# Causal and narrow attention on halves of the array's rows, with per-head waits and moved products

## What is computed

```
x = x + _L0_attn_ref(_layernorm(x), ...)    # causal, 16 heads of 8
...
x = x + _L1_attn_ref(_layernorm(x), ...)    # causal, keys and values from 32 latents
...
x = x + _L2_xattn_ref(_layernorm(x), ctx, ...)   # 512 queries on 77 keys, scores clipped
...
x = x + _L3_xattn_ref(_layernorm(x), ctx, ...)   # 512 queries on 77 keys
...
# the core of each
scores = jnp.einsum('bqhd,bkhd->bhqk', q * scale, k) + bias   # bias: later keys masked, causal ones only
attn_weights = jax.nn.softmax(scores, axis=-1)
attn_output = jnp.einsum('bhqk,bkhd->bqhd', attn_weights, v)
```

## Time and profile before

| | |
|---|---|
| median of 3 runs | 1516.36 us (1514.69 to 1518.23) |
| the profiled execution | 1514.06 us, its span 1512.2 us |
| PE busy | 1418.1 us, 94% of the span |
| DVE / ACT / POOL busy | 955.7 / 674.3 / 346.3 us |
| mean granted clock | 0.979 |

### The profile page before, as it was taken

One profiled execution on the slowest core, in us unless ns is written; L12 is line 12 of the kernel. 1 busy time (PEld: TensorE's weight loads), 2 busy tenths in 40 slices (PEclk: granted clock), 3 DMA queues, 4 the chain that ended last, 5 costly groups with the idle time before them and its releaser, 6 DMA issues. The chain is left out here.

```text
span 1512.2 us, 27644 instructions
## 1 busy us (share of the span) xinstructions
PE 1418.1 (94%) x10790; PEld 890.2 (59%) x10790; DVE 955.7 (63%) x1911; ACT 674.3 (45%) x1651; POOL 346.3 (23%) x372
## 2 busy tenths in 40 slices
PE   8999999999999998998998988989998999999996
PEld 6665574644666656566786857674444555664434
DVE  6676372644366655645668337668888887677755
ACT  4776244324267654524420324533556777750002
POOL 4000031100101010010421202027777665600001
PEclk9999899999899999999999999999999999999998
DMA  3000000421000000000011302010110101399980
GB/s 126 2 2 2 3 2 0 154 72 42 15 2 2 2 2 17 1 20 4 2 60 78 126 11 83 2 43 15 42 42 28 30 15 26 64 223 254 253 213 15
DMA packets 24062, 79.13 MB, mean 52 GB/s; under 512 B 4808, under 2 KB 6646, under 8 KB 23552
## 3 DMA queue, kind: packets, MB, share of 16 engines
q1 hardware_dynamic: 23072, 74.26, 18.0%
q10 hardware_dynamic: 864, 3.15, 0.8%
HBM read 72.11 MB, written 1.08 MB: 48 GB/s over the span
## 5 line engine op out<-in xcount | busy, mean ns | idle before, releaser
L193 PE MATMUL psum<-ident 128*128 128x128 f32 x1392 | 175.7, 284 | 13.0 <-DVE var L143 5.6
L193 PEld LDWEIGHTS psum<-ident 128*128 128x128 f32 x1392 | 167.4, 198 | 20.9 <-DVE var L143 6.6
L475 ACT ACTIVATE pt<-psum,quad_max 128x128 f32<-128x128 f32 (+3 forms) x256 | 133.6, 525 | 68.4 <-DVE quad_max L513 64.4
L184 POOL TENSOR_TENSOR rstd<-var,minus_half 128x4 f32<-128x4 f32 x30 | 30.7, 1023 | 574.5 <-DVE var L143 539.4
L513 DVE TENSOR_REDUCE quad_max<-psum 128x1 f32<-128x128 f32 (+3 forms) x256 | 113.5, 485 | 67.7 <-PE psum L404 67.4
L2733 PE MATMUL psum<-pt,slots 128*128 128x512 f32 x256 | 115.0, 604 | 3.5 <-DVE pt L2886 2.9
L2712 PE MATMUL psum<-slots,xn_t 128*128 128x512 f32 x256 | 113.9, 605 | 3.1 <-DVEq L2857 3.1
L2471 ACT ACTIVATE p<-psum,duo_max 128x512 f32<-128x512 f32 x128 | 86.9, 683 | 43.2 <-DVE duo_max L2506 43.1
L2801 ACT ACTIVATE pt<-psum,p 128x64 f32<-128x64 f32 x256 | 58.0, 393 | 72.5 <-POOL wide L2943 43.7
L2733 PEld LDWEIGHTS psum<-pt,slots 128*128 128x128 f32 x256 | 48.0, 192 | 69.6 <-issue 50.8
L2506 DVE TENSOR_REDUCE duo_max<-psum 128x1 f32<-128x512 f32 x128 | 82.3, 684 | 10.0 <-PE psum L2382 7.8
(11 more groups left out here) (505 smaller groups left out, 2794.1 us busy)
## 6 DMA issues: line engine op xcount, KB each, us to landing
pt<-scratch_out_gates SPq DMA_DIRECT2D x32, 256.0 KB, 12.2
heads<-scratch_out_gates SPq DMA_DIRECT2D x24, 256.0 KB, 14.5
slots<-in_s_l0f SPq DMA_DIRECT2D x8, 514.0 KB, 3.3
wide<-scratch_gates SPq DMA_DIRECT2D x8, 512.0 KB, 7.5
slots<-in_s_l3v SPq DMA_DIRECT2D x8, 512.0 KB, 3.3
context_v<-scratch_out_gates SPq DMA_DIRECT2D x16, 256.0 KB, 18.3
slots<-in_s_l3o ACTq DMA_DIRECT2D x6, 512.0 KB, 10.2
weights<-in_w_l1a SPq DMA_DIRECT2D x1, 2624.0 KB, 9.4
```

The lines of the kernel that those rows point to most:

```text
L193: nc.tensor.matmul(m.ps[bank][:, 0:P], m.ident[:, :], m.ident[:, :], start=True, stop=True, skip_group_check=True)
L475: nc.scalar.activation(m.quad_p[:, i % 2, g, 0:keys], m.ps[g][:, 0:keys], ACT.Exp, bias=m.quad_max[:, i % 2, g:g + 1], accum_out=sum_colum ...
```

## The change

- Two heads of a pair are now each on 64 of the 128 rows (half_rows): head g of the loop lies at rows 64 * (g % 2), with keys copied twice (head_keys, latent_t), once with the odd 32-row quarters zeroed by ScalarE and once with the even ones by VectorE. HEAD_OF maps the loop's order to the heads' places in the output.
- The mask comes as four bf16 products on 64 rows and 64 columns a pair instead of two on all rows and 128 columns.
- Transposes are made of 64 rows each, the two halves into two banks; a step turns two key blocks of four heads (16 instructions) or one (8). VectorE copies out the lower half, ScalarE the upper. The second pair of key blocks is turned after the scores of heads 0 and 1 of the next set.
- Each head's scores wait for that head's exponential alone.
- The spreading product (share) and the projection (ahead) move from behind the values to between the scores of a pair's first and second head: share between heads 2 and 3 of set i when i-3 ended a group, the projection between heads 0 and 1 of set i+1. ScalarE's copy of the projection moves from after head 1's exponential to the end of its step.
- Narrow stages: score tiles of 64 rows, with keys of eight heads in keys_own, and 16 transposes of 64 rows instead of 8 full ones.
- Three constants more are loaded (later, parity, rows8), and one more is cast by ScalarE.

```diff
@@ -392,38 +406,71 @@
     return m.ps[T_BANKS[bank]]
-def quad_scores(nc, pe, m, a, n, heads, q, k, q_ready):
+def quad_scores(nc, pe, m, a, n, heads, q, k, q_ready, between=None):
     b, j, qt = quad_set(n)
     q_ready(pe, b, j, qt)
-    wait(pe, m.quad_exp, GROUP * (a.sets0 + n) - (GROUP - 1 - heads[1] if n else 0))
     keys = (qt + 1) * P
     for g in heads:
+        wait(pe, m.quad_exp, GROUP * (a.sets0 + n) - (GROUP - 1 - g if n else 0))
         nc.tensor.matmul(m.ps[g][:, 0:keys], q(g, b, j, qt), k(g, b, keys), start=True, stop=False)
-    for g in heads:
-        nc.tensor.matmul(m.ps[g][:, keys - P:keys], m.ident_bf[:, :], m.future_bf[:, :], start=False,
-                         stop=True).then_inc(m.quad_scores, 1)
+        if between and g == heads[0]:
+            between()
+    for part in range(2):
+        for g in heads:
+            own, at = half_rows(g % 2), keys - P + 64 * part
+            last = nc.tensor.matmul(m.ps[g][:, at:at + 64], m.later_bf[own, part, :], m.ident_bf[own, own], start=False,
+                                    stop=part == 1)
+            if part == 1:
+                last.then_inc(m.quad_scores, 1)
+def quad_turn(nc, pe, m, a, n, pair):
+    banks = [turn_bank(pe, m, a.turn[n, 2 * pair + half]) for half in range(2)]
+    blocks = pair_keys(n, pair)
+    for kt in blocks:
+        for g in range(GROUP):
+            for half in range(2):
+                own, at = half_rows(half), (kt % 2 * GROUP + g) * 64
+                last = nc.tensor.transpose(banks[half][:, at:at + 64], m.quad_p[own, n % 2, g, kt * P:(kt + 1) * P],
+                                           m.ident[own, own])
+                if kt == blocks[-1] and g == GROUP - 1:
+                    last.then_inc(m.quad_turned, 1)
 def quad_tensor(nc, pe, m, a, q, k, values, q_ready, v_ready, project, ramp):
+    def share(group):
+        pe.wait_ge(m.quad_spread, m.inverted0[a.name] + group + 1)
+        bank = turn_bank(pe, m, a.share[group])
+        for t in range(NQ):
+            last = nc.tensor.matmul(bank[:, t * P:(t + 1) * P], m.quad_wide[:, group % 2, t, :], m.ident[:, :],
+                                    start=True, stop=True)
+        last.then_inc(m.quad_turned, 1)
+    def ahead(group):
+        project(turn_bank(pe, m, a.ahead[group]), group).then_inc(m.quad_turned, 1)
     quad_scores(nc, pe, m, a, 0, (0, 1), q, k, q_ready)
-    for i in range(SETS + 2):
+    for i in range(SETS + 3):
+        shared = (lambda: share((i - 3) // a.group_sets)) if a.ends_group(i - 3) else None
         if i < SETS:
-            quad_scores(nc, pe, m, a, i, (2, 3), q, k, q_ready)
+            quad_scores(nc, pe, m, a, i, (2, 3), q, k, q_ready, shared)
+        elif shared:
+            shared()
         if i < len(RAMP):
             ramp(i)
         n = i - 1
         if 0 <= n < SETS:
-            for kt in range(n % NQ + 1):
-                bank = turn_bank(pe, m, a.turn[n, kt])
-                for g in range(GROUP):
-                    if kt == 0:
-                        pe.wait_ge(m.quad_exp, GROUP * (a.sets0 + n) + g + 1)
-                    last = nc.tensor.transpose(bank[:, g * P:(g + 1) * P], m.quad_p[:, n % 2, g, kt * P:(kt + 1) * P],
-                                               m.ident[:, :])
-                last.then_inc(m.quad_turned, 1)
+            pe.wait_ge(m.quad_exp, GROUP * (a.sets0 + n) + GROUP)
+            quad_turn(nc, pe, m, a, n, 0)
         if i + 1 < SETS:
-            quad_scores(nc, pe, m, a, i + 1, (0, 1), q, k, q_ready)
+            quad_scores(nc, pe, m, a, i + 1, (0, 1), q, k, q_ready,
+                        (lambda: ahead((i + 2) // NQ)) if a.projects(i - 1) else None)
+        if 0 <= n < SETS and key_pairs(n) > 1:
+            quad_turn(nc, pe, m, a, n, 1)
         n = i - 2
         if 0 <= n < SETS:
...
             last.then_inc(m.quad_values, 1)
             if a.ends_group(n):
                 nc.tensor.matmul(m.ps[O_BANK][:, 0:P], m.zeros[:, :], m.ident[:, :], start=False, stop=True,
                                  skip_group_check=True).then_inc(filled(m, f"{a.name}o{group}"), 1)
-                pe.wait_ge(m.quad_spread, m.inverted0[a.name] + group + 1)
-                bank = turn_bank(pe, m, a.share[group])
-                for t in range(NQ):
-                    last = nc.tensor.matmul(bank[:, t * P:(t + 1) * P], m.quad_wide[:, group % 2, t, :], m.ident[:, :],
-                                            start=True, stop=True)
-                last.then_inc(m.quad_turned, 1)
-        if a.projects(i):
-            group = (i + 3) // NQ
-            project(turn_bank(pe, m, a.ahead[group]), group).then_inc(m.quad_turned, 1)
-def quad_take(copy, eng, m, a, n, kt):
+def quad_take(copy, eng, m, a, n, u):
+    pair, half = divmod(u, 2)
+    blocks = pair_keys(n, pair)
     wait(eng, m.quad_values, a.sets0 + n - 1)
-    bank = turn_filled(eng, m, a.turn[n, kt])
-    copy(m.quad_pt[:, n % 2, kt, :], bank).then_inc(m.quad_taken[a.turn[n, kt][0]], 1)
+    bank = turn_filled(eng, m, a.turn[n, u])
+    copy(m.quad_pt[:, n % 2, blocks[0]:blocks[-1] + 1, :].rearrange("p k (g a q) -> p (k g) a q", a=2, q=64)[:, :, half, :],
+         bank[:, 0:len(blocks) * S // 2].rearrange("p (k q) -> p k q", q=64)).then_inc(m.quad_taken[a.turn[n, u][0]], 1)
...
@@ -464,27 +506,27 @@
     for i in range(SETS + 3):
         n = i - 1
-        taken = [kt for kt in range(n % NQ + 1) if kt % 2 == 1] if 0 <= n < SETS else []
+        taken = [2 * pair + 1 for pair in range(key_pairs(n))] if 0 <= n < SETS else []
         if i < SETS:
             b, j, qt = quad_set(i)
             keys = (qt + 1) * P
             if i >= 2:
-                act.wait_ge(m.quad_turned, a.turn[i - 2, (i - 2) % NQ][2] + 1)
+                act.wait_ge(m.quad_turned, a.turn[i - 2, 2 * key_pairs(i - 2) - 1][2] + 1)
             for g in range(GROUP):
                 act.wait_ge(m.quad_negmax, GROUP * (a.sets0 + i) + g + 1)
                 nc.scalar.activation(m.quad_p[:, i % 2, g, 0:keys], m.ps[g][:, 0:keys], ACT.Exp,
                                      bias=m.quad_max[:, i % 2, g:g + 1],
-                                     accum_out=sum_column(g, b, j, qt)).then_inc(m.quad_exp, 1)
+                                     accum_out=sum_column(HEAD_OF[g], b, j, qt)).then_inc(m.quad_exp, 1)
                 if g == 1 and a.ends_group(i - 3):
                     take_output((i - 3) // a.group_sets)
-                if g == 1 and a.projects(i - 1):
-                    take_ahead((i + 2) // NQ)
                 if g >= 2 and taken:
                     quad_take(copy, act, m, a, n, taken.pop(0))
         elif a.ends_group(i - 3):
             take_output((i - 3) // a.group_sets)
-        for kt in taken:
-            quad_take(copy, act, m, a, n, kt)
+        for u in taken:
+            quad_take(copy, act, m, a, n, u)
+        if i < SETS and a.projects(i - 1):
+            take_ahead((i + 2) // NQ)
...
@@ -529,10 +571,11 @@
             dve.wait_ge(m.quad_exp, GROUP * (a.sets0 + n) + GROUP)
             invert(n // a.group_sets).then_inc(m.quad_inverted, 1)
         if 0 <= n < SETS:
-            for kt in range(0, n % NQ + 1, 2):
-                quad_take(nc.vector.tensor_copy, dve, m, a, n, kt)
+            quad_take(nc.vector.tensor_copy, dve, m, a, n, 0)
         if i + 1 < SETS:
             maxima(i + 1, (0, 1))
+        if 0 <= n < SETS and key_pairs(n) > 1:
+            quad_take(nc.vector.tensor_copy, dve, m, a, n, 2)
...
-            nc.scalar.activation(dst[:, j * S:(j + 1) * S], bank[:, :], ACT.Identity,
-                                 bias=bias).then_inc(emptied(m, f"{name}{j}"), 1)
+    for j in range(2):
+        bank = read(m, act, f"l0q{j}")
+        nc.scalar.activation(m.q_t[:, j * S:(j + 1) * S], bank[:, :], ACT.Identity,
+                             bias=w["bq"]).then_inc(emptied(m, f"l0q{j}"), 1)
+    for j in range(2):
+        bank = read(m, act, f"l0k{j}", 1)
+        nc.scalar.activation(m.head_keys[0][:, j * S:(j + 1) * S], bank[:, :], ACT.Identity, bias=w["bk_even"],
+                             scale=m.parity[:, 0:1]).then_inc(emptied(m, f"l0k{j}"), 1)
     def take_output(b):
...
     head_queries(0)
+    for j in range(2):
+        copied(m, dve, f"l0k{j}")
+        bank = read(m, dve, f"l0k{j}", 1)
+        nc.vector.tensor_scalar(m.head_keys[1][:, j * S:(j + 1) * S], bank[:, :], m.parity[:, 1:2], w["bk_odd"], ALU.mult,
+                                ALU.add).then_inc(emptied(m, f"l0k{j}"), 1)
     for j in range(2):
         bank = read(m, dve, f"l0v{j}")
...
@@ -1697,9 +1762,9 @@
                 else:
                     wait(pe, m.negmax_ready, a.s0 + k - 1)
                 for x in range(2):
-                    rows = own(2 * half + x)
+                    rows = slice(64 * x, 64 * x + 64)
                     last = nc.tensor.matmul(m.ps[2 * (k % 2) + x][:, 0:GROUP * SC], m.q_t[rows, b * S + qt * P:b * S + (qt + 1) * P],
```

(14 more changed lines are left out.)

117 lines of the change are left out of this document (78 added, 39 removed).

## The result

The changed kernel takes **1508.30 us** (median of 4 runs, 1506.73 to 1509.97) against 1516.59 before (4 runs): ratio 0.9946, 95% interval [0.9929, 0.9963]. It is faster, but by 8 us, not by the forecast 34, and the time lies above the range (1467 to 1499). A second set gave 1510.77 (12 runs) and 0.9969 [0.9947, 0.9990]. The profiled execution took 1508.48, span 1506.7, mean granted clock 0.972 (0.979 before).

A forecast was written before the change was run, and what follows sets the result against it. TensorE's sequence was taken to bound the causal stages until other engines and the score-bank chain do. First causal stage -17.6, second -7.8, narrow -6.6 and -2.4, together -34.4, gave 1482 us; forecast 1474 to 1490, range 1467 to 1499.

The forecast's parts named there:

- TensorE's own work: First causal stage, TensorE's round: transposes 2.75, scores 4.8, mask 1.0, value products 3.2, together 11.8 us.
- What is late next: First causal stage: VectorE 10.7, ScalarE 11.6, one-bank chain 11.0; longest by set 12.6, so a round of 12.7 us.
- rival B: Causal stages: the chain and the queues bind, rounds of 13.9 and 17.0 us, time 1498; chance 0.18.
- Spreading and projection between the heads: Second causal stage: heads can't run side by side, +0.65 and +0.87; round 15.6 us on TensorE, 16.4 forecast.
- Rival C: Causal stages: pairs come apart, each costing its streams twice, +4.36 and +2.8 us a round, time 1524; chance 0.04.
- Starts: Start of both causal stages: next projection also waits for VectorE's copy of the keys, some 0.8 us at each.
- Head by head: Causal stages: waiting for each head's exponential separately costs TensorE nothing alone, since the mask needs both heads' exponentials anyway.
- Narrow stages: Half transposes shorten the later stage's round from 5.90 to 4.95 us, -6.6 in all; the earlier stage -2.4.
- The clock: Sign of being wrong: granted clock, 1.00 in both stretches of the table, falls with TensorE's new waits; no size given.

The follow-up runs named there:

- cuts on different engines: Kernel with both scores of a pair before spreading and projection; maxima, value products, ScalarE's copies cut to 128 keys: 1482.68, 1492.04, 1502.78 us alone, 1468.66 together.
- moving VectorE's copy: Kernel with both scores of a pair before spreading and projection, plus VectorE's first-turn copy between the maxima of heads 2 and 3: 1495.88 us, ratio 0.9878.
- three moves made for this loop: Both scores before spreading and projection, plus VectorE's copy between maxima; value products behind scores of heads 2 and 3; or both: 1495.88, 1498.24, 1525.03 us.
- both scores ahead: Changed kernel with spreading and projection issued behind both scores of their pair instead of between the heads: 1499.56 us, ratio 0.9906; again 1502.05, 0.9909.

## Why the prediction was wrong, point by point

**TensorE's own work: right.** 16 half transposes take 0.53 (109.91 to 110.44, the next group's start), forecast 0.55. The round without its waits, 13.86 - 1.58 - 0.6, is 11.7; forecast 11.8. The rule of the Trainium skill (TensorE: Matmul & The Clock Gate, LDWEIGHTS) that was set aside, by which alone 16 loads would take an estimated 1.7 us, does not give the price of these loads on alternating halves.

**What is late next: the step that failed.** TensorE's work was right and its waits were not: forecast 12.7 - 11.8 = 0.9 a round, measured 2.2. The prediction read the chain at one bank, scores, maximum, exponential, summed it to 11.0, took 12.6 as the sum of the longest by set, and went for 12.7 with a ceiling of 13.9 "a quarter of the idle share more". But the loop that exists doesn't stay in one bank: it takes value products and turns out of TensorE's queue, copies out of VectorE's and ScalarE's, 8.0 us on TensorE's side, 4.1 on VectorE's and 1.8 or so on ScalarE's, and comes to 13.85. TensorE waits for it: 1.19 and 0.39 for VectorE's copies, 0.6 for ScalarE's exponential. It can probably be written down from the code's four queues and the durations of the earlier trace rows; that was not tried. Eight rounds 1.16 too long are 9.3 us. It is **rival B** in this stage, to its number of 13.9; in the second stage its 17.0 was passed (17.57), and its total of 1498 would still have been missed.

**Spreading and projection between the heads: price right, place wrong.** I costed the split at 1.52 and counted it on TensorE, with 0.8 for waits on top (16.4). Measured it is 1.52 too, but on top of a round that was 16.05 and not 14.9: 8 x 1.17 = 9.4 us missed. That the two figures agree is partly luck. The forecast is TensorE's lost overlap alone; the measured one is a whole round's, in which VectorE and ScalarE stand idle for up to 2.78. Rival C's mechanism, a pair that comes apart because its second head waits, shows in one pair of eight in the first stage (118.58 to 120.15) and costs nothing there: with one wait for the pair it stays together behind a wait of 0.54, and the round is 13.89.

**Starts: right.** +1.1 in the first stage in this profile, some +0.8 on average, and +0.9 in the second; forecast +0.8 each. **Head by head: right** (0.03 a round).

**Narrow stages: right at full clock.** 2.5 gained (forecast 2.4) and 5.7 (forecast 6.6; the round is 5.11, forecast 4.95). **The clock: named as a sign of being wrong, and not priced.** In the profiled run it kept 6.2 us of the narrow gain (0.8 more is the forecast's own excess). In the first causal stage it cost an estimated 1.9, against the same kernel's second profile, which has falls of its own: 0.85 in one round (14.88 against 14.03) and 1.05 from the last round's first exponential to the next normalization (28.52 against 27.47). In the untouched stage behind it cost 1.4.

The sum by spans: forecast -34.4, measured -5.5, so 28.9 are missing. The first causal stage has 12.8 of them: 9.3 by the rounds, 1.9 by the clock, 1.6 not assigned. Behind it 1.6 were lost, 1.4 by the clock. The second causal stage has 10.9: 9.4 by the rounds, 1.5 not assigned. The narrow stages have 7.0: 6.2 by the clock and 0.8 of forecast. The rest gave 3.5 back, 3.0 of it at 1028 to 1036. So about two thirds of the miss (18.7) are the rounds, with the loop and the split, and a third (9.5) is the clock.

**Still open:** why the clock falls where it does. At full clock the later narrow stage had TensorE busy 81% (51.95 of 63.83), with falls 83%, so its busy share over the stage doesn't tell them apart. And why the value products gave 0.84 of the 1.33 that stand on the loop.

## What to carry to other kernels

When an edit takes work off the engine that is full, write down the loop through all queues before you name the next bound: start at a wait, go back through whatever stands ahead in each in-order queue, until the same instruction of the round before. Work on that loop counts, and cuts on different engines add up (0.91, 0.84 and 0.32 alone, 2.17 together), but only until another wait takes over: moving VectorE's copy took 0.76 us off the waits read and gave 0.16. The busy share of an engine says little (3.0 us off VectorE gave 0.9). Check the reading by a move before you count on it: of three moves made for this loop, none met its forecast in the first stage. Two instructions that run side by side on halves of the array are one unit: put nothing between them, and their finishing steps neither. A gain of under 1% shows in stage rounds long before it shows in the time of a kernel whose clock moves.

## What the runs showed of the hardware

The granted clock fell in stretches of 4 to 16 us at different places from program to program, and from one profiled execution to another of the same program (the first causal stage with both scores ahead: end at 148.9 and 152.8), to as low as 0.50 (148 to 152 us of the changed kernel). The share not granted, times the span, is 32 us in the profile before (0.979 of 1512.2), 42 in the changed kernel's (0.972 of 1506.7) and 27 in the one with VectorE's copy in between (0.982 of 1488.0). That last one is the fastest of its four executions; they average 0.977. The 10 us between the first two are more than the change gained (8), though not all of them are on the path.
